# Message passing and mixture-of-experts kernel: in the last stage, the first loads of the second choices go from ScalarE to SyncE

## What is computed

```python
x = x + gnn(layernorm(x))            # 6250 nodes x 256, 100000 edges, segment sum
x = x + ffn(layernorm(x))

def ffn(x):                          # EX = 16 experts, 2 of them for each node
    gate_logits = x @ gate_w + gate_b
    topk_vals, topk_idx = top_k(gate_logits, 2)
    topk_w = softmax(topk_vals)
    h = relu(x @ w1[e] + b1[e])
    expert_out = h @ w2[e] + b2[e]
    moe = sum over the two choices of topk_w * expert_out[choice]
    y = x + moe
    return (y - mean(y)) / sqrt(var(y) + EPS) * gamma + beta
```

## Time and profile before

| | us |
|---|---|
| median of 3 runs | 2032.62 (2030.38 to 2033.19) |
| the profiled execution | 2029.74 |
| its span | 2027.7 |
| last stage in it, from ScalarE's first load to the end | 88 |
| TensorE busy, whole span | 1467.2 (72%) |
| GpSimd busy | 1142.7 (56%) |
| VectorE busy | 955.5 (47%) |
| ScalarE busy | 635.3 (31%) |

### The profile page before, as it was taken

The page is one execution under the profiler, slowest core; times in us unless marked ns, Lnnn a source line. Parts: engine busy times, 40 slices in busy tenths (PEclk is TensorE's granted clock), DMA queues, the critical chain, the costliest instruction groups (busy, mean ns, idle before and its releaser), DMA issues. The chain is left out here.

```text
span 2027.7 us, 33634 instructions
## 1 busy us (share of the span) xinstructions
PE 1467.2 (72%) x7822; PEld 1158.9 (57%) x7823; DVE 955.5 (47%) x2240; ACT 635.3 (31%) x1710; POOL 1142.7 (56%) x1156
## 2 busy tenths in 40 slices
PE   7006888476777777777777777776259999999974
PEld 4005888354544545445545445454149999988853
DVE  8999999433233332332333333333663333333347
ACT  4624999000010101001001001010545444444466
POOL 1001443577777777777777777777215554544435
PEclk9558999778788887887778888888579999999987
DMA  5102000233333333333333333333642222243366
GB/s 177 36 18 74 7 6 6 72 104 104 103 105 104 105 104 103 105 105 104 103 104 104 103 104 104 104 104 104 155 132 83 70 81 95 91 147 125 108 200 215
DMA packets 107299, 201.64 MB, mean 99 GB/s; under 512 B 19972, under 2 KB 68731, under 8 KB 107128
## 3 DMA queue, kind: packets, MB, share of 16 engines
q0 software_dynamic: 52672, 139.93, 23.5%
q1 hardware_dynamic: 39704, 42.83, 6.4%
q10 hardware_dynamic: 14880, 18.35, 2.8%
HBM read 165.17 MB, written 35.86 MB: 99 GB/s over the span
## 5 line engine op out<-in xcount | busy, mean ns | idle before, releaser
L837 POOL DMA_INDIRECT hbuf<-xn_rows,ix x832 | 797.4, 958 | 266.6 <-issue 235.3
L886 PE MATMUL bank<-hbuf,picks 128*128 x2032 | 654.9, 463 | 280.9 <-SPq L825 280.3
L886 PEld LDWEIGHTS bank<-hbuf,picks 128*128 128x128 f32 x2032 | 416.4, 223 | 498.4 <-issue 443.6
L865 DVE TENSOR_SCALAR picks<-iota_two,marks 128x256 f32<-128x256 f32 x832 | 334.7, 446 | 688.4 <-PE bank L886 674.3
L954 ACT ACTIVATE agg<-bank 128x256 f32<-128x256 f32 x49 | 18.8, 383 | 865.6 <-PE bank L886 865.6
L398 POOL DMA_INDIRECT edge_groups<-work,dest_i x56 | 80.7, 1441 | 279.5 <-DVE work L622 266.7
L751 PE MATMUL bank<-work 128*128 128x192 bf16 x1568 | 144.9, 249 | 116.4 <-DVE work L615 116.4
L1518 PEld LDWEIGHTS bank<-rowsT,w_sb 128*128 128x128 f32 x1744 | 211.9, 193 | 28.9 <-issue 24.1
L1518 PE MATMUL bank<-rowsT,w_sb 128*128 128x128 f32 x1744 | 215.2, 277 | 17.7 <-issue 17.7
L1454 POOL DMA_INDIRECT expert_out<-y_sb,to_i x112 | 111.1, 992 | 185.6 <-DVE from_i L1551 105.2
L1528 PE MATMUL bank<-w_sb,hT 128*128 128x256 f32 x872 | 206.8, 380 | 0.0
(11 more groups left out here) (259 smaller groups left out, 1380.6 us busy)
## 6 DMA issues: line engine op xcount, KB each, us to landing
w_sb<-in_L_ffn_w_dram ACTq DMA_DIRECT2D x28, 512.0 KB, 4.7
hbuf<-xn_rows,ix POOLq DMA_INDIRECT x832, 2.7
xn_rows<-xn SPq DMA_DIRECT2D x11, 896.0 KB, 4.0
x<-in_x_dram SPq DMA_DIRECT2D x6, 896.0 KB, 11.0
ya<-expert_out SPq DMA_DIRECT2D x5, 896.0 KB, 5.4
yb<-expert_out SPq DMA_DIRECT2D x5, 896.0 KB, 8.2
xn_rows<-x SPq DMA_DIRECT2D x3, 896.0 KB, 4.1
out_dram<-o SPq DMA_DIRECT2D x5, 512.0 KB, 3.0
```

The costliest lines, as they stand in the source:

```text
L837: pool.indirect_dma_start(hbuf[:, 1 + j, k, :], None, xn_dram, bass.IndirectOffsetOnAxis(ap=ix[:, 2 * j + k:2 * j + k + 1], axis=0)).then_ ...
L865: s = v.tensor_scalar(picks[:, j % 2, k, :], iota_two[:], marks[:, 0, 2 * j + k:2 * j + k + 1], marks[:, 1, 2 * j + k:2 * j + k + 1], ALU. ...
L886: m = nc.tensor.matmul(bk[q][:, 0:D], picks[:, j, k, q * P:(q + 1) * P], hbuf[:, ds(place + j, 1), k, :].rearrange("p s d -> p (s d)"), st ...
```

## The change

The second choices' loads of batches 0 and 1 (two pieces and one whole) leave ScalarE's program and stand at the head of last_sync, behind a wait for a new semaphore, all_sent, that ScalarE raises once when it has seen all real scatters land. ScalarE keeps the three loads of the first choices. The number and sizes of the transfers stay the same. The shapes of the later loads are unchanged; load is only rewritten with one.

```diff
+        all_sent = sem("all_sent")
...
+        def one(engine, t, k):
+            to, there = ((ya, ya_in), (yb, yb_in))[k]
+            engine.dma_start(to[t % 2][:], y_dram[t * WB * P + k * NP:(t + 1) * WB * P + k * NP, :].rearrange("(w p) d -> p w d", p=P)).then_inc(there[t % 2], 16)
+
+        def first_parts(engine, to, k, there):
+            engine.dma_start(to[:, 0:EARLY, :], y_dram[k * NP:EARLY * P + k * NP, :].rearrange("(w p) d -> p w d", p=P)).then_inc(early_in, 16)
+            engine.dma_start(to[:, EARLY:WB, :], y_dram[EARLY * P + k * NP:WB * P + k * NP, :].rearrange("(w p) d -> p w d", p=P)).then_inc(there, 16)
+
         def load(engine, t):
-            q = t % 2
-            for k, (to, there) in enumerate(((ya[q], ya_in[q]), (yb[q], yb_in[q]))):
-                engine.dma_start(to[:], y_dram[t * WB * P + k * NP:(t + 1) * WB * P + k * NP, :].rearrange("(w p) d -> p w d", p=P)).then_inc(there, 16)
+            for k in range(2):
+                one(engine, t, k)
 
         def last_sync(sp):
+            sp.wait_ge(all_sent, 1)
+            first_parts(sp, yb[0], 1, yb_in[0])
+            one(sp, 1, 1)
...
-            for to, k in ((ya[0], 0), (yb[0], 1)):
-                act.dma_start(to[:, 0:EARLY, :], y_dram[k * NP:EARLY * P + k * NP, :].rearrange("(w p) d -> p w d", p=P)).then_inc(early_in, 16)
-            for to, k, there in ((ya[0], 0, ya_in[0]), (yb[0], 1, yb_in[0])):
-                act.dma_start(to[:, EARLY:WB, :], y_dram[EARLY * P + k * NP:WB * P + k * NP, :].rearrange("(w p) d -> p w d", p=P)).then_inc(there, 16)
-            load(act, 1)
+            act.sem_inc(all_sent, 1)
+            first_parts(act, ya[0], 0, ya_in[0])
+            one(act, 1, 0)
```

## The result

| | us |
|---|---|
| before, median of 7 runs | 2032.62 (2029.94 to 2035.85) |
| changed kernel, median of 7 runs | 2039.61 (2038.22 to 2041.01) |
| ratio | 1.0034, 95% interval 1.0024 to 1.0044 |
| changed kernel, profiled execution | 2039.21, span 2037.3 |

The change makes the kernel slower by 7.0 us, 4.9 to 8.9 us by the interval. The forecast was 6.3.

What follows compares the result with a forecast made beforehand. The last stage's first loads lie on the path to the end, with ScalarE pacing its batches. First product 10.4 us late less 4.1 of slack gives 6.3, so 2032.6 + 6.3 = 2038.9 us; range 2036.5 to 2041, chance 0.68.

Steps and rivals of the forecast that it cites:

- SyncE isn't there when ScalarE is: Head of SyncE's last stage: its loop's waits for surplus gathers delay the moved yb loads by over ten microseconds.
- N1: Start of ScalarE's normalising of batch 1 in the last stage, 1968.15 before; forecast 6.3 us late, everything behind moving with it.
- SyncE's first load at 1951.2: Last stage: SyncE issues its first yb load at 1951.2, within bounds of 1950.9 and 1954.17.
- The early piece lands 3.7 us after its issue: First yb piece of batch 0, alone on its way: lands at 1954.9, making TensorE's first product 10.4 us late.
- Batch 0 takes 8.4 us from cold: TensorE's first batch of the last stage: 8.4 us, of which 4.0 at the lower clock.
- batch 0 has 4.09 us of slack: Last stage: batch 0 can be 4.09 us late at no cost if batch 1's loads aren't late too.
- No gap in front of batch 1: TensorE between batches 0 and 1: yb loads land by 1958.6, needed at 1963.3, so it runs through without waiting.
- Everything behind N1 moves whole: Last stage after batch 1: ScalarE keeps 8.36 us a batch, 41.81 us to the normalising of batch 6.
- The rule of the Trainium skill: Engines share the same 16 DMA engines; issuing from two saves only issue time, here a gain of 0.51 us.
- Slack of 7 us or more behind batch 0: Rival in the last stage: batch 0's delay is mostly hidden, result -0.5 to +3 us; within 0.2%, chance 0.16.
- Gathers that land at once: Rival at SyncE's loop: it leaves early and N1 falls to its floor, -4.1 us, 2028.5; chance 0.04.
- SyncE as late as before: Rival at SyncE's loop: held to 1954.17, N1 10.1 us late, 2042.7; chance 0.12, shared with TensorE slower from cold.

Runs made afterwards that it cites:

- e1: Changed kernel with SyncE's three yb loads moved ahead of its waits for the last group of four tiles; 2395.89 us against 2394.71 of before, ratio 1.0002.
- e6: Changed kernel without the last group's four surplus gathers; 2040.0 us against 2034.87 of before, ratio 1.0026.
- e10: Changed kernel itself, run again on a chip where the kernel before takes 2393.96 us; 2397.52 us, ratio 1.0016.
- e4a: Kernel before, with TensorE's first product of the last stage also waiting for SyncE's y_gone at 114; 2037.21 us against 2034.87, ratio 1.001.
- e4b: Kernel before, with TensorE's first product of the last stage also waiting for SyncE's y_gone at 116; 2399.83 us against 2394.71, ratio 1.0019.
- e7: Changed kernel without the four surplus gathers and with SyncE's yb loads ahead of its last four waits; 2030.92 us against 2034.87 of before, ratio 0.9981.
- e3: Changed kernel with only yb of batch 1 issued by SyncE, all other first loads by ScalarE; 2398.09 us against 2394.71 of before, ratio 1.0015.
- e5: Kernel before without the last group's four surplus gathers; 2031.83 us against 2034.87 of before, ratio 0.999.

## Why the prediction was right, step by step

- *SyncE isn't there when ScalarE is, since its loop waits for surplus gathers.* Right. The chain of the changed kernel runs over the last gather, and e1 brings SyncE's load and N1 back by the place in the program alone. What e6 adds is that the surplus scatters would hold SyncE nearly as long; the prediction named the gathers only.
- *SyncE's first load at 1951.2, that is 11.65 us behind ScalarE's.* It was 12.15. The last gather took 4.54 us to the end of SyncE's wait where I took the 3.6 of an idle queue as the floor and 0.3 more. ScalarE's queue was nearly empty by then, as forecast; the backlog of indirect transfers was what I had too small. Between 1950 and 1954 of the changed kernel's trace the indirect queue was still moving 0.41 MB, when ScalarE's had 0.03 MB left:

```profile
q0 software_dynamic: 158, 0.41, 50.9%
q10 hardware_dynamic: 31, 0.03, 1.9%
```

- *The early piece lands 3.7 us after its issue.* It was 3.1, alone on free queues. Next come SyncE's loads in the changed kernel, KB and median us to landing:

```profile
yb<-expert_out SPq DMA_DIRECT2D x1, 896.0 KB, 7.7
yb<-expert_out SPq DMA_DIRECT2D x1, 512.0 KB, 4.1
yb<-expert_out SPq DMA_DIRECT2D x1, 384.0 KB, 3.1
```

  The two errors, +0.5 and -0.6 us, cancel: the first product was put at 15.35 us behind ScalarE's first load and stood at 15.34. That it fits so closely is luck; in e10 it stood at 15.04.
- *Batch 0 takes 8.4 us from cold.* 8.6. The clock in the changed kernel (columns as in rows 7) stood at half over most of a longer stretch, 4.8 us against 4.0 in rows 7:

```profile
1957.10:1961.90 4.80, 4.76 (x12) 3.84 (x13) 1.18 (x3) 1.39 (x4) 0.00 (x0) 0.51 0.75 260
1961.90:1966.00 4.10, 4.10 (x21) 3.62 (x20) 3.27 (x9) 3.00 (x9) 0.00 (x0) 1.00 0.01 3
```

- *From the last sum of batch 0 to N1 ScalarE needs 11.19 us, and batch 0 has 4.09 us of slack.* 35.15 - 23.96 = 11.19 in the changed kernel, and e4a and e4b measured the slack without moving a load: at least 4.35 - 0 and 10.26 - 6.14 = 4.12.
- *No gap in front of batch 1, its loads in time.* Right; it starts before VectorE has taken the last sum of batch 0. Batch 2 was held 2.56 us for load 2 where I had put about one, without effect on N1:

```profile
1974.33 0.67 PE L1349 MATMUL bank<-ya,shares 128*128 128x256 f32 x2 [2.56 <-DMA yb<-expert_out]
```

- *Everything behind N1 moves whole, at 8.36 us a batch.* Nearly. The 41.81 us weren't five equal steps: in before the fourth was longer and the fifth shorter, and that the sum is 5 times 8.36 is chance. Four of the five steps hold, 8.36, 8.36, 8.51 and 8.36 us before and 8.36, 8.36, 8.52 and 8.36 after, but the last was 8.23 before and 8.99 after. This is the mis-sized term, 0.77 us. In batch 6 ScalarE waits for VectorE and VectorE for TensorE, and TensorE's speed there is its clock. The three stretches are batch 6 of before, of the changed kernel and of e7:

```profile
2000.30:2005.80 5.50, 5.50 (x26) 4.85 (x27) 4.82 (x18) 4.46 (x11) 2.71 (x1) 1.00 0.23 80
```

```profile
2008.97:2016.50 7.53, 7.53 (x27) 6.33 (x28) 6.60 (x22) 4.60 (x11) 4.60 (x2) 0.77 0.25 90
```

```profile
2001.56:2010.50 8.94, 8.94 (x28) 7.32 (x28) 6.33 (x15) 3.63 (x8) 4.77 (x2) 0.66 0.33 118
```

  Ahead of them TensorE had been idle for 1.94, 2.53 and 4.19 us, the latter two for the load of batch 6. In before the clock stayed at 1.00, in the two others it fell, and the last step became 8.99 and 11.26 us. Batch 6 itself didn't start later in the changed kernel: 32.02 us behind N1, where it was 32.15 in before. TensorE had only come to the end of batch 5 sooner. Over all traces the picture is coarse: with 1.94 and 1.50 us idle (the two of before) the step is 8.23, in the ten others that have such a wait, 2.53 to 4.19 us of it, 8.76 to 11.26, but not in the order of the idle times (3.03 us and 10.26 in e3, 3.86 us and 8.79 in e1). The prediction had named a pace other than 8.36 as a sign of being wrong that would give some of the loss back; it took some more.
- *The rule of the Trainium skill* ("DMA: Bandwidth & Descriptors", section "Issuing engines are not separate DMA queues"), by which the split saves only issue time. By e1, which is that split without the wait, the runs agree with it as far as they can tell: +0.5 us (-1.9 to +3.1). For the changed kernel it gave a small gain, and the measured 7 us loss lies outside what it speaks of.
- *The size.* 6.3 us forecast, 6.55 at N1 in the first trace (5.88 between the two second traces) and 0.77 behind it; 7.0 measured on that chip. On e10's chip the total was 3.8 us, a little under the forecast's low end of 4.1. So the mechanism is on firmer ground than the size.
- *The rivals.* Slack of 7 us or more behind batch 0: excluded by e4b. Gathers that land at once: they took longer than on an idle queue, and even without them (e6) SyncE came at 10.55. SyncE as late as before: in part; its first load came 2.5 us earlier than in before, of the 3.3 us that were possible.

## What to carry to other kernels

A load that is moved to another engine's queue starts when that engine's program gets there, not when its semaphore allows; look up what stands ahead of it there, above all waits for transfers whose data nobody needs. What such a delay costs is read from the stage's pace maker: here 4.1 of 10.4 us were slack against batch 0, while batch 1 had none. A way to test such a claim without moving anything is to hold the first consumer by a wait on a later event (e4a, e4b), and the versions that are a little better than both came from taking away work that only kept the bookkeeping even (e5, ratio 0.999, and e7, 0.9981, which can't be told from each other).

## What the runs showed of the hardware

- Scatters and gathers of GpSimd fall back when a long run of loads from ScalarE is queued: the last scatter of e6 was issued 3.4 us behind ScalarE's first load, and SyncE, which waited for it, issued its next load at 10.55, with 1.83 MB of ya in the queues. A gather took 3.6 us to SyncE's wait ahead of those loads and the last one 4.54 us behind 1.83 MB of them. SyncE's first load came at 12.0, 13.5 and 15.3 us with 1.83, 2.2 and 2.75 MB on ScalarE's queue, surplus gathers included, and at 14.6 in before with 3.67 MB. So it didn't grow any more beyond 2.75 MB. For 2.2 and 2.75 MB these are single traces.
- Half a megabyte less of indirect transfers (e5) let batch 1 start 2.1 us sooner, 14.71 for 16.79, in a stretch in which the queues moved some 300 GB/s. At that rate the bytes alone are 1.7 us, an estimate from these rows, so they explain most of it.
- One program took 2032 to 2035 us on some chips and 2394 on two others, and by the table the last stage was no slower on those. The mean granted TensorE clock was 0.85 and 0.79, but that needn't be the cause. From 600 to 900 us GpSimd did 167 gathers in e1, of 955 ns, where it did 239 in the changed kernel, of 957 ns, and TensorE stood 139 us in place of 77 ahead of the products of the same line. What grew is waiting, and what the engines wait for there isn't settled.
